# A decoder kernel's expert blocks loaded six ahead, and two GpSimd reciprocal roots moved behind the first wide product

## The chip, the cores and the metric

One Trainium2 chip, one of its cores. The metric is device time of one launch in microseconds (us). TensorE runs matmuls and transposes, VectorE and ScalarE do elementwise work and copy products out of PSUM, GpSimd does some elementwise work and issues the indirect (row by row) DMAs, SyncE (SP) issues the plain DMAs.

## What is computed

A post-norm decoder of two layers on x of 16 x 64 tokens of 128 features (1024 rows, held as 8 tiles of 128 rows). Cut to its skeleton:

```python
x = _layernorm(x + self_attention_0(x))
x = _layernorm(x + cross_attention_0(x, ctx))
x = _layernorm(x + moe(x))                 # 8 experts, the best 2 of each token
x = _layernorm(x + wide_attention(x))      # 16 heads of 64
x = _layernorm(x + cross_attention_1(x, ctx))
x = _layernorm(x + ternary_ffn(x))

def _moe_forward(x_flat):
    top_v, top_i = jax.lax.top_k(x_flat @ gate_w.T, 2)
    probs = softmax(top_v)
    for each expert e:
        hidden = silu(x_flat @ wg[e].T) * (x_flat @ wu[e].T)
        out += weight_of_e[:, None] * (hidden @ wd[e].T)
```

## The kernel before

Three parts follow each other. A first stream takes the 16 tiles of the two first attentions (`pre`), then the expert part (class `Routed`) runs, then a second stream (`post`) takes 24 tiles: 8 of the wide attention (class `Wide`), 8 of the second cross attention, 8 of the ternary feed-forward. Each engine has its own instruction queue, written out by hand; semaphores (`Mark`s) order the engines.

**The expert part.** The tokens are scattered by indirect DMA into a table in HBM, `routed_rows`, sorted by expert. 23 blocks of 128 rows are then worked off. For block j SP loads its rows into one of four buffers `XG[j % 4]` (L1458); TensorE transposes them (`block_pe`, L1472) two steps ahead of use; ScalarE copies the transpose out (L1478); GpSimd brings the expert's weights (L1488); TensorE makes the gate product (L1500, 8 instructions in the trace), the up product (L1508, 8) and, one block behind, the down product (L1531, 8); ScalarE makes the SiLU (L1516), VectorE the product of both (L1523) and the copy of the result to `YS` (L1539), and SP stores it back to `routed_rows` (L1466). At step n of its loop TensorE runs: transpose of block n+2, gate n, up n, down n-1. Some of VectorE's work on the ternary weights is put between blocks (L941 and others), after blocks 5 to 12.

SP's loop (`rows_sp`) issues four loads, then for each j: the load of block j+4, the wait for block j's copied result, the store of block j. `load(j)` waits for the transpose of block j-4, which frees the buffer.

**The gathering.** When all stores have landed, GpSimd gathers for each token tile t the two expert rows of each token (`gather`, L1662, two DMAs a tile). VectorE combines them with x and makes mean and variance (`combine`, L1670 to L1678), GpSimd makes the reciprocal root of the variance in two short instructions (`rsqrt`, L1683 and L1685), VectorE applies it (`apply`, L1690), TensorE and ScalarE turn the tile (L1698, L1703). VectorE combines and applies tiles 0 and 1 in the expert part; tiles 2 and 3, 4 and 5, 6 and 7 stand at the end of steps 1, 2 and 3 of its second stream (`post_dve`). GpSimd has all eight reciprocal roots in the expert part, ahead of its second stream.

**The second stream.** Step j of the stream holds, for the wide tiles: on TensorE the scores of tile j-2 (L835), the q and k products of tile j-1 (L808, 32 instructions in the trace), the v products of tile j-2 (L821, 16), the transposes of the probabilities P of tile j-3 (L426, 8), the product of P with V of tile j-4 (L852), then turned token tiles (L1698; tiles 4 and 5 at the end of step 3). The probabilities come about so: VectorE takes the row maximum (L400) and subtracts it (L406), ScalarE makes the exponentials (L416), VectorE sums them (L893) and takes reciprocals (L897), and GpSimd multiplies P by them (`shares_pool`, L887). This last product of tile 0 is the first wide product of P; it is GpSimd's first work in its second stream, at step 3.

Of the kernel before, what the change touches and what calls it, by code (L numbers as in the profile page):

```python
# [17 lines left out]
NT = BATCH * SEQ // P  # L18
# [14 lines left out]
BLOCKS = (2 * BATCH * SEQ + 8 * (P - 1)) // P  # L33
# [44 lines left out]
def decoder_kernel(nc, A, out):  # L78
    with ExitStack() as ctx:
# [8 lines left out]
        class Mark:  # L88
# [8 lines left out]
            def at(self, n):  # L97
                return self.sem, self.base + n

        def bc(ap, axis, n):  # L100

            shape = list(ap.shape)
            shape.insert(axis, n)
            return ap.unsqueeze(axis).to_broadcast(shape)
# [146 lines left out]
        class Transposes:  # L251
# [20 lines left out]
            def copies(self, eng, part, some=None):  # L272
                for g in some or range(len(self.groups)):
                    if g % 2 != part:
                        continue
                    _, blocks, dst = self.groups[g]
                    eng.wait_ge(self.mm, g + 1)
                    src = PS[:, self.banks[g % len(self.banks)], 0:sum(k for _, k in blocks)]
                    if part == 0:
                        eng.activation(dst, src, ACT.Copy).then_inc(self.copied[0], 1)  # L280
                    else:
                        eng.tensor_copy(dst, src).then_inc(self.copied[1], 1)
# [25 lines left out]
        class Norm:  # L308
# [18 lines left out]
            def rsqrt(self, pool, i):  # L327

                pool.wait_ge(*self.mv.at(i + 1))
                pool.tensor_scalar(ve[:, i % 2, :], mv[:, i % 2, 1:2], LN_EPS, None, ALU.add).then_inc(self.ve.sem, 1)  # L330
                pool.wait_ge(*self.ve.at(i + 1))
                pool.tensor_tensor(rstd[:, i % 2, :], ve[:, i % 2, :], half[:, :], ALU.pow).then_inc(self.rstd.sem, 1)  # L332
# [10 lines left out]
        class Stage:  # L343
# [48 lines left out]
            def rsqrt_pool(self, pool, job):  # L392
                self.norm.rsqrt(pool, job.i)
# [721 lines left out]
        def stream_of(*stages):  # L1115
            tiles = []
            for st in stages:
                for i in range(NT):
                    tiles.append(Tile(st, i, len(tiles), tiles))
            return tiles  # L1120
# [6 lines left out]
        def summed(tiles, j):  # L1127

            t, w = at(tiles, j - 5), at(tiles, j - 4)
            return w if w and w.stage.wide else t if t and not t.stage.wide else None  # L1130

        def turned(tiles, j):
            return summed(tiles, j - 1)
# [109 lines left out]
        def stream_pool(pool, tiles, extra):  # L1243
            for j in range(len(tiles) + DEPTH):
                t = at(tiles, j - 3)
                if t:
                    t.stage.shares_pool(pool, t)
                b = at(tiles, j - 1)
                if b:
                    b.stage.blocks_pool(pool, b)  # L1250
                b = at(tiles, j)
                if b:
                    b.stage.cos_pool(pool, b)
                if t:
                    t.stage.hidden_pool(pool, t)
                r = summed(tiles, j)
                if r:
                    r.stage.rsqrt_pool(pool, r)
                x = turned(tiles, j)
                if x:  # L1260
                    x.stage.bias_pool(pool, x)
                extra(pool, j)

# [3 lines left out]
        ROUTED = {0: 0, 2: 1, 4: 2, 5: 3}  # L1269


        class Routed:
# [174 lines left out]
            def rows_sp(self, sp):  # L1447

                sp.wait_ge(*self.map.at(12))
                _, at = nc.values_load_multi_w_load_instructions(  # L1450
                    bi[0:1, 1, 0:BLOCKS], engines=[mybir.EngineType.SP], min_val=0, max_val=ROWS - P,
                    skip_runtime_bounds_check_because="counts of 128 rows summed on the chip, whose largest sum ROWS holds")
                sp.wait_ge(s_sc, 16 * 2 * NT)

                def load(j):
                    if j >= 4:
                        sp.wait_ge(*self.xt_mm.at(j - 3))
                    sp.dma_start(XG[:, j % 4, :], routed[bass.ds(at[j], P), :]).then_inc(s_xg[j % 4], 16)  # L1458

                for j in range(4):  # L1460
                    load(j)
                for j in range(BLOCKS):
                    if j + 4 < BLOCKS:
                        load(j + 4)
                    sp.wait_ge(*self.ycp.at(j + 1))
                    sp.dma_start(routed[bass.ds(at[j], P), :], YS[:, j % 3, :]).then_inc(s_ys[j % 3], 16)  # L1466

# [165 lines left out]
            def pool(self, pool):  # L1633
                self.scatter(pool, len(GROUPS) - 1)
                pool.wait_ge(*self.w_cp.at(3 * EXPERTS))
                pool.wait_ge(*self.map.at(8))
                _, e = nc.values_load_multi_w_load_instructions(
                    bi[0:1, 0, 0:BLOCKS], engines=[mybir.EngineType.Pool], min_val=0, max_val=EXPERTS - 1,
                    skip_runtime_bounds_check_because="a sum of seven comparisons, each 0 or 1")
                for j in range(2, BLOCKS):  # L1640
                    self.bring_pool(pool, j, e[j])
                    if j in (6, 9, 12):
                        pool.wait_ge(s_wide, 16)
                        pool.tensor_copy(WQKV[:, j // 3 - 2, :], WRAW[:, j // 3 - 2, :]).then_inc(s_sep, 1)
                for k in range(3):
                    pool.wait_ge(s_ys[k], 16 * len(range(k, BLOCKS, 3)))
                self.gather(pool, 0)
                self.gather(pool, 1)
                self.rsqrt(pool, 0)
                self.gather(pool, 2)  # L1650
                self.rsqrt(pool, 1)
                for t in range(2, NT, 2):
                    self.gather(pool, t + 1)
                    if t + 2 < NT:
                        self.gather(pool, t + 2)
                    self.rsqrt(pool, t)
                    self.rsqrt(pool, t + 1)


            def gather(self, pool, t):  # L1660
# [49 lines left out]
        moe = Routed(a1.norm)  # L1710
# [6 lines left out]
        pre, post = stream_of(a0, a1), stream_of(wide, a2, fc)  # L1717
# [60 lines left out]
            if late and k in ROUTED:  # L1778
                moe.place(dve, ROUTED[k])

        def pre_pool(pool, j):
            k = j - DRAIN
            if k in ROUTED:
                moe.scatter(pool, ROUTED[k])

        TURNED = {(1, True): (1,), (2, True): (2, 3), (3, True): (4, 5), (4, False): (6, 7)}
# [15 lines left out]
                for t in (2 * j, 2 * j + 1):  # L1802
                    moe.apply(dve, t)

        def no_pool(pool, j):
            pass

        def load_biases(eng, b):

# [58 lines left out]
        @block.gpsimd  # L1868
        def _(pool):
            pool.memset(half[:, :], -0.5).then_inc(s_half, 1)  # L1870

            pool.memset(zero[:, :], 0.0).then_inc(s_zt, 1)
            pool.memset(VB[:, :, :, :, :, :], 0.0).then_inc(s_z, 1)
            pool.wait_ge(s_cst, 16)
            pool.wait_ge(s_z, 1)
            for b in range(2):
                for a in range(2):
                    pool.tensor_copy(VB[:, :, :, b, a, DH], bc(cst[:, C_HALF + a:C_HALF + a + 1], 1, 3).to_broadcast([P, 3, PAIRS]))\
                        .then_inc(s_z, 1)
            pool.wait_ge(s_half, 1)  # L1880
            for h in range(2):
                pool.wait_ge(s_x[h], 16)
            pool.wait_ge(s_b[0], 16 * NB)
            stream_pool(pool, pre, pre_pool)
            moe.pool(pool)
            stream_pool(pool, post, no_pool)

        @block.scalar
        def _(act):
# [51 lines left out]
```

## Time and profile before

| | us |
|---|---|
| median of 3 timed runs | 412.69 |
| lowest and highest of them | 410.81, 412.75 |
| the profiled execution's own time | 409.98 |
| span of the profile (first to last instruction) | 408.0 |
| mean granted TensorE clock | 0.946 of full |

| engine | busy us | share of the span |
|---|---|---|
| TensorE (PE) | 347.2 | 85% |
| VectorE (DVE) | 252.6 | 62% |
| GpSimd (POOL) | 186.3 | 46% |
| ScalarE (ACT) | 183.7 | 45% |

In the profile's time the expert blocks run from about 133 to 208 us, the gathering begins at 211 us, and step 3 of the second stream lies from about 240 to 258 us. A busy share is a mean over stages; the chain of waits tells which engine ended each stretch last. "Idle before" in a row is the time in which the engine stood still right before it, and the name behind the arrow is what ended that.

### The profile page before, as it was taken

To read this page: it belongs to the slowest core of one execution; us is meant where nothing else is said; L and a number is where in the kernel's file an instruction comes from. 1 tells how busy PE (TensorE), PEld (TensorE's weight loads), DVE (VectorE), ACT (ScalarE), POOL (GpSimd) and SP (SyncE) were. 2 spreads that over 40 slices of the span, in tenths; PEclk is the share of its full clock that TensorE was granted. 3 is DMA by queue.
4 is the path that set the end of the run, shared out by engine and by line. 5 is a ranking of instruction groups with operands and counts; after the bars stand their busy time and mean duration, and the time that the engine had idled before them with its cause. 6 is when DMAs were issued, how large, how long until landed. Compare 5 with 4: busy or idle time off the path is not lost.

```text
span 408.0 us, 9801 instructions
## 1 busy us (share of the span) xinstructions
PE 347.2 (85%) x3718; PEld 263.3 (65%) x3718; DVE 252.6 (62%) x592; ACT 183.7 (45%) x386; POOL 186.3 (46%) x267
## 2 busy tenths in 40 slices
PE   3889899998970899898986874899999989999892
PEld 2556666665870889898975561756667565667572
DVE  1799988896554125732353776435566567887894
ACT  2466676664672422222221251433454335667541
POOL 1767666655455245433227633102222247452673
PEclk9999999996996799999996988699999999999998
DMA  6799900000381011111111100000000000000000
GB/s 199 238 307 300 292 2 2 2 2 28 96 261 39 27 53 40 39 40 53 29 31 42 34 19 2 0 2 2 2 2 2 2 2 2 2 2 2 2 26 26
DMA packets 35938, 22.95 MB, mean 56 GB/s; under 512 B 4142, under 2 KB 33846, under 8 KB 35766
## 3 DMA queue, kind: packets, MB, share of 16 engines
q1 hardware_dynamic: 34582, 19.63, 16.7%
q0 software_dynamic: 1024, 2.10, 1.7%
q8 instruction: 30, 0.49, 0.5%
q10 hardware_dynamic: 288, 0.62, 0.5%
q14 instruction: 14, 0.11, 0.1%
HBM read 14.60 MB, written 7.73 MB: 55 GB/s over the span
## 4 chain that ended last, share of the span: by engine, by line
PE 58%; DVE 14%; issue 8%; POOL 7%; ACT 5%; DMA 5%; SPq 1%; POOLq 0%; DVEq 0%; ACTq 0%
PE banks L426 7%; PE banks L821 6%; PE banks L546 5%; PE banks L523 4%; PE banks L1500 4%; PE banks L1508 4%; PE banks L1531 4%; PE banks L808 4%; DMA XG<-routed_rows 3%; PE banks L852 3%; POOL KB L670 2%; PE banks L530 2%; DVE mx L400 2%; PE banks L495 2%; PE banks L507 2%
## 5 line engine op out<-in xcount | busy, mean ns | idle before, releaser
L330 POOL TENSOR_SCALAR ve<-mv 128x1 f32<-128x1 f32 x40 | 10.6, 265 | 93.8 <-DVE mv L325 93.8
L670 POOL TENSOR_TENSOR KB<-KT,cst 128x512 f32<-128x512 f32 x48 | 49.3, 1047 | 7.5 <-DVE KT L630 5.6
L435 ACT ACTIVATE PT<-banks 128x512 f32<-128x512 f32 x64 | 34.9, 595 | 33.3 <-PE banks L426 32.3
L1523 DVE TENSOR_TENSOR PT<-banks,PR 128x512 f32<-128x512 f32 x23 | 15.9, 691 | 46.6 <-PE banks L1508 40.0
L400 DVE TENSOR_REDUCE mx<-banks 128x16 f32<-128x1024 f32 x32 | 38.7, 1209 | 7.9 <-PE banks L530 5.6
L858 ACT ACTIVATE U<-banks 128x512 f32<-128x512 f32 x40 | 23.9, 597 | 42.5 <-PE banks L821 22.1
L426 PE MATMUL banks<-cst,PR 128*128 128x128 f32 x256 | 36.6, 289 | 6.5 <-POOL PR L887 6.5
L1488 POOL COPY U<-WALL 128x1024 f32 x21 | 21.8, 1040 | 43.8 <-PE banks L1508 42.2
L426 PEld LDWEIGHTS banks<-cst,PR 128*128 128x128 f32 x256 | 29.0, 146 | 10.2 <-POOL PR L887 7.6
L808 PE MATMUL banks<-XT,WQKV 128*128 128x128 f32 x256 | 34.9, 300 | 0.4 <-ACT XT L1703 0.4
L416 ACT ACTIVATE PR<-PR 128x1024 f32<-128x1024 f32 x32 | 33.8, 1057 | 3.1 <-DVE PR L410 2.8
L821 PE MATMUL banks<-WALL,XT 128*64 128x512 f32 x128 | 32.1, 611 | 3.3 <-DVE U L858 2.9
L808 PEld LDWEIGHTS banks<-XT,WQKV 128*128 128x128 f32 x256 | 33.1, 210 | 1.5 <-ACT XT L1703 0.7
L858 DVE COPY U<-banks 128x512 f32<-128x512 f32 x24 | 16.5, 689 | 24.7 <-PE banks L821 18.0
L523 PE MATMUL banks<-KB,QS 64*64 64x512 f32 x192 | 28.7, 651 | 2.8 <-DVE PR L410 1.5
L410 DVE TENSOR_TENSOR PR<-banks,mx 128x1024 f32<-128x1024 f32 x24 | 29.4, 1224 | 0.8
L336 DVE TENSOR_SCALAR X<-R,mv,rstd 128x128 f32<-128x128 f32 x40 | 19.2, 479 | 16.0 <-POOL rstd L332 15.9
L546 PE MATMUL banks<-VB,PT 128*64 128x18 f32 x768 | 27.0, 214 | 0.0
L546 PEld LDWEIGHTS banks<-VB,PT 128*64 128x64 f32 x768 | 24.6, 139 | 3.1 <-issue 0.6
L1500 PE MATMUL banks<-XGT,U 128*128 128x128 f32 x184 | 25.4, 283 | 0.0
L1508 PE MATMUL banks<-XGT,U 128*128 128x128 f32 x184 | 25.2, 282 | 0.0
L1531 PE MATMUL banks<-WALL,PT 128*128 x184 | 24.4, 276 | 0.6 <-DVE YS L1539 0.6
(181 smaller groups left out, 699.1 us busy)
## 6 DMA issues: line engine op xcount, KB each, us to landing
routed_rows<-zero SPq DMA_DIRECT2D x1, 4544.0 KB, 19.1
U<-in_L_ffn_wg_dram SPq DMA_DIRECT2D x8, 256.0 KB, 5.0
U<-in_L_ffn_wu_dram SPq DMA_DIRECT2D x8, 256.0 KB, 5.3
U<-in_L_ffn_wd_dram SPq DMA_DIRECT2D x8, 256.0 KB, 6.0
U<-in_L_attn_W_qkv_dram SPq DMA_DIRECT2D x1, 1536.0 KB, 22.7
XG<-routed_rows SPq DMA_DIRECT2D x23, 64.0 KB, 1.8
routed_rows<-YS SPq DMA_DIRECT2D x23, 64.0 KB, 1.6
cst<-shape_constants ACTq DMA_DIRECT2D x1, 537.0 KB, 4.6
```

The lines of the kernel that those rows point to most:

```text
L400: dve.tensor_reduce(mx[:, n % 2, :], s, AX.X, ALU.max).then_inc(self.max.sem, 1)
L426: t = pe.transpose(PS[:, B_PT + m, P * (r % 4):P * (r % 4 + 1)], PR[:, n % 2, P * r:P * (r + 1)], ident)
L435: act.activation(PT[:, n % 2, 4 * m:4 * m + 4, :].rearrange("p r q -> p (r q)"), PS[:, B_PT + m, :], ACT.Copy).then_inc(self.pt.sem, 1)
L523: pe.matmul(PS[q, B_S + g, :], QS[f, n % 3, q], KB[f, n % 2, b].rearrange("p h k -> p (h k)"), start=True, stop=False)
L546: m = pe.matmul(PS[64 * b:64 * b + 64, B_Y, w * r:w * (r + 1)], PT[:, n % 2, r, 64 * b:64 * b + 64], VB[:, n % 3, r, b].rearrange("p a e - ...
L670: pool.tensor_tensor(KB[:, n % 2, b], bc(KT[:, n % 2, b, :], 1, 8), bc(cst[:, C_HEAD:C_HEAD + 8], 2, SEQ), ALU.mult).then_inc(self.kb.sem, 1)
L808: m = pe.matmul(PS[:, bank, P * k:P * (k + 1)], WQKV[:, f // 2, P * u:P * (u + 1)], XT[:, P * i:P * (i + 1)], start=True, stop=True)
L821: m = pe.matmul(PS[64 * a:64 * a + 64, bank, :], XT[:, SEQ * (2 * i + b):SEQ * (2 * i + b + 1)], WVO[:, a, 4 * g:4 * g + 4, :].rearrange(" ...
L858: return eng.activation(o, s, ACT.Copy) if part == 0 else eng.tensor_copy(o, s)
L1500: m = pe.matmul(PS[:, j % 2, P * c:P * (c + 1)], WE[:, j % 3, 0, P * c:P * (c + 1)], XGT[:, j % 3, :], start=True, stop=True)
L1508: m = pe.matmul(PS[:, 2 + j % 2, P * c:P * (c + 1)], WE[:, j % 3, 1, P * c:P * (c + 1)], XGT[:, j % 3, :], start=True, stop=True)
L1531: m = pe.matmul(PS[:, 7, 0:P], HT[:, j % 2, c, :], WALL[:, e, 2, P * c:P * (c + 1)], start=(c == 0), stop=(c == CH - 1))
```

## The change

SP issues six loads ahead of its loop rather than four, and in the loop the load of block j+6 rather than j+4 stands in front of block j's store. The four buffers and what `load` waits for stay. GpSimd's reciprocal roots of token tiles 6 and 7 leave the expert part and stand in step 3 of the second stream, behind `shares_pool` of tile 0. For that the function that a stream calls for extra work on GpSimd is called at two places in a step, with a flag as on the other engines; what it did in the first stream stays at the late place.

```diff
@@ stream_pool
                     t.stage.shares_pool(pool, t)
+                extra(pool, j, False)
                 b = at(tiles, j - 1)
...
-                extra(pool, j)
+                extra(pool, j, True)
@@ rows_sp
-                for j in range(4):
+                for j in range(6):
                     load(j)
                 for j in range(BLOCKS):
-                    if j + 4 < BLOCKS:
-                        load(j + 4)
+                    if j + 6 < BLOCKS:
+                        load(j + 6)
                     sp.wait_ge(*self.ycp.at(j + 1))
@@ Routed.pool
                     if t + 2 < NT:
                         self.gather(pool, t + 2)
-                    self.rsqrt(pool, t)
-                    self.rsqrt(pool, t + 1)
+                        self.rsqrt(pool, t)
+                        self.rsqrt(pool, t + 1)
@@
-        def pre_pool(pool, j):
+        def pre_pool(pool, j, late):
             k = j - DRAIN
-            if k in ROUTED:
+            if late and k in ROUTED:
                 moe.scatter(pool, ROUTED[k])
@@
-        def no_pool(pool, j):
-            pass
+        def post_pool(pool, j, late):
+            if j == 3 and not late:
+                for t in (NT - 2, NT - 1):
+                    moe.rsqrt(pool, t)
```

SP's queue at the head of its block loop, before (each load is an address row and a DMA row; `block_transposed` is TensorE's transpose, `expert_output_copied` VectorE's copy of the result):

```order
L1458 DMA XG<-routed_rows 128x128
L1458 ISA [waits block_transposed]
L1458 DMA XG<-routed_rows 128x128
L1466 DMA routed_rows<-YS 128x128 [waits expert_output_copied]
L1458 ISA [waits block_transposed]
L1458 DMA XG<-routed_rows 128x128
L1466 DMA routed_rows<-YS 128x128 [waits expert_output_copied]
```

The same place after (the lines of the file are one higher):

```order
L1459 DMA XG<-routed_rows 128x128
L1459 ISA [waits block_transposed]
L1459 DMA XG<-routed_rows 128x128
L1459 ISA [waits block_transposed]
L1459 DMA XG<-routed_rows 128x128
L1459 ISA [waits block_transposed]
L1459 DMA XG<-routed_rows 128x128
L1467 DMA routed_rows<-YS 128x128 [waits expert_output_copied]
```

Ahead of the first store stand the loads of blocks 4, 5 and 6 where the load of block 4 alone stood, and from there each load is two stores earlier than it was.

GpSimd's queue from the gathers of the last token tile (tile 7) to the first wide products of P, before:

```order
L1662 DMA KB<-routed_rows,pos 128x128 x2
L1683 TENSOR_SCALAR ve8<-mv8 128x1 [waits variance_made]
L1685 TENSOR_TENSOR rstd8<-ve8,half 128x1 [waits eps_added]
L1683 TENSOR_SCALAR ve8<-mv8 128x1 [waits variance_made]
L1685 TENSOR_TENSOR rstd8<-ve8,half 128x1 [waits eps_added]
L887 TENSOR_TENSOR PR<-PR,rs 128x1024 [waits reciprocals_made] x2
```

and after:

```order
L1663 DMA KB<-routed_rows,pos 128x128 x2
L887 TENSOR_TENSOR PR<-PR,rs 128x1024 [waits reciprocals_made]
L1684 TENSOR_SCALAR ve8<-mv8 128x1 [waits variance_made]
L1686 TENSOR_TENSOR rstd8<-ve8,half 128x1 [waits eps_added]
L1684 TENSOR_SCALAR ve8<-mv8 128x1 [waits variance_made]
L1686 TENSOR_TENSOR rstd8<-ve8,half 128x1 [waits eps_added]
L887 TENSOR_TENSOR PR<-PR,rs 128x1024 [waits reciprocals_made]
```

Of the two products of P that stood behind the four short instructions, the one of tile 0 now stands ahead of them. TensorE's, VectorE's and ScalarE's queues are unchanged.

## Rows read from the trace of the kernel before

**Rows 1.** The page's chain that ended last, its shares of the span by line.

```profile
PE banks L426 7%; PE banks L821 6%; PE banks L546 5%; PE banks L523 4%; PE banks L1500 4%; PE banks L1508 4%; PE banks L1531 4%; PE banks L808 4%; DMA XG<-routed_rows 3%; PE banks L852 3%; POOL KB L670 2%; PE banks L530 2%; DVE mx L400 2%; PE banks L495 2%; PE banks L507 2%
```

**Rows 2.** Groups from 138 to 198 us: count, busy us, mean ns, idle before.

```profile
L1472 PE MATMUL banks<-cst,XG 128*128 128x128 f32 x19 | 5.8, 305 | 4.4 <-DMA XG<-routed_rows 4.4
...
L941 DVE TENSOR_SCALAR PT<-FCW,gam 128x512 f32<-128x512 f32 x2 | 3.1, 1608 | 0.0
```

**Rows 3.** Busy time by stretch: us, PE, PEld, DVE, ACT, POOL, clock, DMA share, GB/s.

```profile
138.00:198.00 60.00, 55.62 (x480) 54.01 (x480) 25.15 (x50) 16.61 (x38) 24.47 (x23) 0.99 0.15 41
```

**Rows 4.** TensorE's timeline in the blocks: start us, us, line, operation [idle before].

```profile
138.54 0.33 PE L1472 MATMUL banks<-cst,XG 128*128 128x128 f32 x1
...
141.38 0.27 PE L1472 MATMUL banks<-cst,XG 128*128 128x128 f32 x1
141.49 1.06 PE L1500 MATMUL banks<-XGT,U 128*128 128x128 f32 x8
...
143.28 1.06 PE L1531 MATMUL banks<-WALL,PT 128*128 x8
144.33 0.33 PE L1472 MATMUL banks<-cst,XG 128*128 128x128 f32 x1
...
198.29 0.33 PE L1472 MATMUL banks<-cst,XG 128*128 128x128 f32 x1
```

**Rows 5.** SP's timeline in the blocks: the load of block 5.

```profile
142.46 0.34 SPq L1458 DMA_DIRECT2D XG<-routed_rows  x1
```

**Rows 6.** The line of the block loads: from issue to landing.

```profile
DMA to landing us min/median/max: 1.7/1.8/3.4
```

**Rows 7.** Timeline of all engines around step 3 of the second stream.

```profile
237.85 0.44 PE L1698 MATMUL banks<-cst,X 128*128 128x128 f32 x1 [2.05 <-ACT XT L1703]
...
241.19 0.96 POOL L1662 DMA_INDIRECT KB<-routed_rows,pos  x1 [0.30 <-issue]
241.24 0.25 DVE L897 RECIPROCAL rs<-mx 128x16 f32<-128x16 f32 x1
...
244.44 3.87 PE L821 MATMUL banks<-WALL,XT 128*64 128x512 f32 x16
...
250.34 0.25 POOL L1683 TENSOR_SCALAR ve<-mv 128x1 f32<-128x1 f32 x1 [8.19 <-DVE mv L1678]
...
252.39 1.90 POOL L887 TENSOR_TENSOR PR<-PR,rs 128x1024 f32<-128x1024 f32 x1
252.46 1.92 DVE L1690 TENSOR_SCALAR X<-R,mv,rstd 128x128 f32<-128x128 f32 x1 [0.76 <-POOL rstd L1685]
254.35 1.97 PE L426 MATMUL banks<-cst,PR 128*128 128x128 f32 x8 [6.03 <-POOL PR L887]
...
258.58 1.99 PE L835 MATMUL banks<-U 64*64 64x64 f32 x64
...
264.86 3.87 PE L821 MATMUL banks<-WALL,XT 128*64 128x512 f32 x16
```

**Rows 8.** The line of `apply`: duration ns min/median/max.

```profile
L1690 DVE TENSOR_SCALAR X<-R,mv,rstd x8: 345/371/1915, 217.3 to 252.5; 128x128 f32<-128x128 f32 x8
```

**Rows 9.** Timeline of all engines two steps on, at steps 4 and 5.

```profile
272.02 1.09 PE L426 MATMUL banks<-cst,PR 128*128 128x128 f32 x8
...
273.05 1.16 PE L835 MATMUL banks<-U 64*64 64x64 f32 x64
...
276.44 1.90 POOL L887 TENSOR_TENSOR PR<-PR,rs 128x1024 f32<-128x1024 f32 x1 [2.50 <-DVE rs L897]
...
277.47 1.23 DVE L406 TENSOR_TENSOR PR<-banks,mx 128x1024 f32<-128x1024 f32 x1
278.02 1.08 PE L821 MATMUL banks<-WALL,XT 128*64 128x512 f32 x4
```

**Rows 10.** Busy time by stretch, columns as in rows 3: PE and its clock.

```profile
238.00:239.00 1.00, 1.00 (x29) 0.78 (x32) 0.85 (x4) 0.28 (x1) 0.79 (x2) 0.50 0.00 0
...
249.00:250.00 1.00, 0.00 (x0) 0.00 (x0) 0.93 (x4) 0.00 (x0) 0.00 (x0) 1.00 0.00 0
...
276.00:288.00 12.00, 11.76 (x154) 8.28 (x153) 6.79 (x12) 5.06 (x9) 2.69 (x3) 1.00 0.01 3
```

More of the change, by code:

```diff
@@ L1885, in _ @@
             moe.pool(pool)
-            stream_pool(pool, post, no_pool)
+            stream_pool(pool, post, post_pool)
         @block.scalar
```

## The prediction

> **What bounds the kernel now.** I read the chain that ended last first: TensorE's lines lead it, but one DMA has 3% of the span, some 12 us, the loads of the expert blocks [rows 1]. So the blocks come next, from 138 to 198 us. TensorE is busy 55.62 of 60.00 us there at full clock (0.99), VectorE 25.15, ScalarE 16.61, GpSimd 24.47 [rows 3]; no engine but TensorE is near its limit, and what holds TensorE up is named in its group of transposes: 4.4 us idle until a load had landed [rows 2]. The second place is step 3 of the second stream. TensorE's v products end at 244.44 + 3.87 = 248.31, and its next work, the transposes of P of wide tile 0, starts at 254.35 after 6.03 us of idleness that GpSimd's product of P ended [rows 7]. That product started at 252.39. Its own input, the reciprocals on VectorE, was ready at 241.24 + 0.25 = 241.49 [rows 7]. What held GpSimd was the instruction ahead in its queue: the reciprocal root of token tile 6 waited 8.19 us for the variance, made by VectorE only at 250.3, since VectorE combines tiles 6 and 7 at the end of step 3 [rows 7]. TensorE thus waited for a small piece of work that neither it nor the product needs.
>
> **Part 1, the loads.** Removed: nothing. Moved: each load, past two stores on SP's queue. Without a wait TensorE needs per block 0.11 us for the transpose (141.38 to 141.49) and 0.895 us for each of three products (141.49 to 143.28 holds two), 2.79 us together [rows 4]. The down product that starts at 143.28 is over by 144.17, yet the next transpose starts at 144.33: its load was issued at 142.46, 1.87 us earlier, and a load lands after 1.8 us in the median [rows 4 to 6]. So even the loads that seem to be on time are late by 0.1 to 0.2 us, and one that takes 3.4 us costs the whole excess [rows 6]. From the transpose of block 3 at 138.54 to that of block 22 at 198.29 are 19 blocks in 59.75 us; 19 x 2.79 = 53.0, so 6.7 us are lost [rows 4]. I take off 0.4 us, an estimate for the small ternary product that stands in there once and for transposes that start a little slower: **6.3 us** come back. The bounds are 4.4 us (the idle time that the group names) and 6.7 us.
>
> Does the new place give enough lead? Load j+6 is issued where load j+4 was, and is needed two blocks later: 1.87 + 2 x 2.79 = 7.45 us of lead, against 3.4 us for the slowest landing seen [rows 4 to 6]. Its wait, the transpose of block j+2, is passed by then: TensorE makes it at step j, and SP gets to this load only behind the store of block j-1, whose down product is also step j's last. So the added wait holds no store back, and the stores queued behind it keep their time. What is late next? VectorE has the ternary weights between blocks, two instructions of 3.1 us together [rows 2], longer than one block. Its mean without these two is (25.15 - 3.1) / 20, 1.1 us a block [rows 2, 3], so two blocks need 3.1 + 2.2 = 5.3 us of 5.58: it fits, barely, and may cost some tenths; the lower bound of 4.4 us covers that. The last stores, the gathers and all that follows hang on the last down product and move up with it.
>
> **Part 2, the reciprocal roots.** The four short instructions stay, 0.25 us and the like each; they go behind the product of P, and that takes 1.90 us [rows 7]. GpSimd is free of its last gather at 241.19 + 0.96 = 242.15, has the reciprocals since 241.49, and ends the product near 244.1. TensorE comes to the transposes of P at 248.31, 4 us later, so GpSimd is out of the way. What is late next is then the chain inside step 3: transposes of P, two copies on ScalarE, the exponentials of tile 1, the turned token tiles 4 and 5 (TensorE waits for ScalarE's copy of the one before it can make the other, as one step earlier, 2.05 us idle [rows 7]), and the scores of tile 2. In the trace this takes 258.58 - 254.35 = 4.23 us [rows 7]; the transposes ran at half clock there, 1.97 us against 1.09 at full clock [rows 9], so I put 4.23 - 0.88 = 3.35 us. The clock was still full (1.00) at 249 to 250 [rows 10]. The scores of tile 2 then start at 248.31 + 3.35 = 251.7 rather than 258.58: **6.9 us** come back. The bounds: 6.0 us (should the chain take its 4.23) and 7.3 us.
>
> Does VectorE follow? It is done with combining both tiles and applying tile 6 by 252.46 - 0.76 = 251.70 and applies tile 7 from 252.46, as before [rows 7]. In the trace that took 1.92 us beside GpSimd's product, against a median of 0.37 [rows 7, 8]. After the change no product runs there and it is over at 252.85. Then tile 1's sum and reciprocals and tile 2's maximum and subtraction (L893, L897, L400, L406; 0.25 and 1.23 us by [rows 7, 9], the sum and the maximum taken as long as the subtraction, an estimate) end near 256.8. The second v product of tile 2 needs VectorE's copy behind these, by about 251.7 + 4.97 + 1.08 = 257.8 (score start to first v product and its length, [rows 9]); the copy fits with little to spare. If VectorE's 1.92 us stayed, TensorE would lose about 1 us. From there each stage runs at TensorE's pace, 11.76 us busy of 12.00 [rows 10], and the gain has nothing to vanish into.
>
> The Trainium skill (SBUF — State Buffer, section Who interferes with whom) has it that VectorE and GpSimd share one port pair, and that whoever holds it blocks the other for its whole instruction, if the VectorE instruction has two SBUF inputs or runs in a two-port mode. By that page the moved product sets `apply` free and holds up none of its new neighbours, as the subtraction reads PSUM. The trace agrees: the subtraction took 1.23 us fully beside a product of 1.90 us, and the product kept its length [rows 9]. Were every VectorE instruction blocked, the product of tile 0 would delay VectorE by under 2 us at 242 us, where ScalarE needs the result only some 6 us later, and that of tile 1 would cost TensorE some 1.5 us.
>
> **The clock.** Scores to first v product of tile 2 took 264.86 - 258.58 = 6.28 us after the long idleness, at half clock in part, against 278.02 - 273.05 = 4.97 at full clock [rows 7, 9]: 1.3 us to win if the clock stays up. The idleness left in step 3 is some 1.7 us. The nearest row is that of one step earlier: 2.05 us idle, then clock 0.50 [rows 7, 10]. It is a little longer, so I take half, **0.6 us**, bounds 0 and 1.3. Moving the idle stretches may also lengthen or shorten the other half-clock stretches, an estimate of 1.5 us either way.
>
> **The sum.** 6.3 + 6.9 + 0.6 = 13.8 us. Against the profiled execution's own 409.98 (span 408.0 and 1.98 around it) that gives 396.2 us. The timed runs' median, 412.69, lies 2.7 us above that execution, and all three are above it; carried over, the time is **398.9 us**.
>
> **Rivals.**
> 1. A new wait takes a part of the gain: VectorE, packed in step 3 and between the blocks, becomes the one that is waited for. For it: the margins above are of 0.3 to 1 us, and VectorE is busy 0.93 us of the one from 249 to 250 [rows 10]. Against it: it is under half busy in the blocks [rows 3]. Price: part 1 at 4.4, part 2 down to 4, no clock gain, sum 8.4: 404.3 us.
> 2. The loads go on holding TensorE, because their landing time is no constant but grows with the loads and stores that are in flight together. Then part 2 alone pays: 412.69 - 7.5 = 405.2 us. Against it: the lead grows fourfold.
> 3. The change doesn't do what it says, or both waits hide others of equal length (TensorE's wait for the product of P might hide a second one, for ScalarE): within 2 us of 412.7. Against it: the reciprocals were 10.9 us old when the product of P began, and nothing else in TensorE's queue changes place.
> 4. Slower: the stores. A load now lies between stores whose landing frees the three `YS` buffers and at the end releases the gathers. Were loads and stores together to land in over 7.45 us, TensorE would wait again at each block, for the excess. To eat the 7.5 us of part 2 over 17 blocks it takes 0.44 us each, a landing of 7.9 us, and for 2.5 us more than before 8.0 us, over four times the median [rows 6]: 415 us.
>
> **How the numbers follow.** The forecast has 0.74 (395 to 402), rival 1 0.12, rival 2 0.07, rival 3 0.04, rival 4 0.03. The low end is the sum's upper bounds, 6.7 + 7.3 + 1.3 = 15.3, and 0.5 to 1.5 us of clock elsewhere, set against a value between 409.98 and 412.69: 394.5 us. The high end takes in rival 1: 404.5 us. A measurement of this kernel tells a change of over 0.5%, 2.1 us, from none. Faster by more than that: 0.93; within 0.5%: 0.04; slower by more: 0.03.
>
> **What the changed profile would show.** Part 1: the block transposes have no idle time before them that ends with a load, apart from the first; each block takes 2.8 us; loads are issued some 7 us before their transpose. Part 2: the product of P of tile 0 starts some 10 us before the combining of tile 6 ends; the transposes of P follow the v products without a gap; `apply` of tile 7 takes 0.4 us; the clock at half rate appears, if at all, only behind the turned tiles. I am wrong if TensorE's idle time in step 3 reappears under VectorE's or ScalarE's name, or if the blocks stay at 2.9 us and more with another releaser.

## The result

| | before | changed |
|---|---|---|
| timed runs, median (lowest to highest), us | 411.75 (408.19 to 412.75) | 394.88 (394.38 to 395.17) |
| profiled execution's own time, us | 409.98 | 394.38 |
| span of the profile, us | 408.0 | 392.4 |
| mean granted TensorE clock | 0.946 | 0.960 |

The ratio is 0.960, with a 95% interval of 0.954 to 0.967: 4.0% less. 398.9 us was forecast, 3.3% less, with a range from 394.5 to 404.5. In three later comparisons, where the kernel before takes 415.5 to 418.0 us, the same pair gave 0.966, 0.967 and 0.965 (below). So 3.4% is what the change gives as a rule, which is about the 13.8 us that were forecast; the first comparison had some 2 us more, and the ledger below shows from where.

The page's chain by line, for [rows 1] (from the expert part on, lines of the changed file are one higher), no longer has the block loads:

```profile
PE banks L426 7%; PE banks L821 6%; PE banks L546 6%; PE banks L1501 5%; PE banks L1509 5%; PE banks L1532 5%; PE banks L523 5%; PE banks L852 3%; DVE mx L400 3%; PE banks L808 3%; PE banks L495 2%; PE banks L530 2%; PE banks L507 2%; DVE mx L893 2%; PE banks L1308 2%
```

The blocks first. The group of VectorE's two ternary instructions from 138 to 192 us (columns as in [rows 2]):

```profile
L941 DVE TENSOR_SCALAR PT<-FCW,gam 128x512 f32<-128x512 f32 x2 | 3.1, 1608 | 0.0
```

They are as long as before. The view of the tile `XG` shows the block transposes of the whole kernel (duration ns min/median/max, first and last start us; then idle time by releaser, with its count):

```profile
L1473 PE MATMUL banks<-cst,XG x23: 272/273/476, 131.2 to 189.6; 128*128 128x128 f32 x23
its engine sat idle before it (us, times) until:
  DMA XG<-routed_rows: 17.6, 4
  ACT XGT L1479: 0.9, 2
...
DMA to landing us min/median/max: 1.7/1.8/3.1
```

The median transpose takes 273 ns where rows of 0.33 us stood between those of 0.27 [rows 4], and landing has the median that it had [rows 6]. The 17.6 us (counted on the weight side and on the matmul side) lie ahead of the first three blocks, when the scatter has just ended. TensorE's timeline shows the pace (start us, us, line, operation):

```profile
136.38 0.27 PE L1473 MATMUL banks<-cst,XG 128*128 128x128 f32 x1
...
139.17 0.27 PE L1473 MATMUL banks<-cst,XG 128*128 128x128 f32 x1
...
189.62 0.27 PE L1473 MATMUL banks<-cst,XG 128*128 128x128 f32 x1
```

From block 3 to block 22 it is 189.62 - 136.38 = 53.24 us, against 59.75 [rows 4]; one block takes 2.79 us. SP issues a load long ahead:

```profile
140.25 0.34 SPq L1459 DMA_DIRECT2D XG<-routed_rows  x1
```

That is the load of block 7. Block 7 is transposed four blocks after the one at 136.38, at 147.54: 7.3 us of lead where there were 1.87 us [rows 5]. The wait that this load adds holds no store back, as the rows of the second store show:

```profile
142.16 0.29 DVE L1540 COPY YS<-banks 128x128 f32<-128x128 f32 x1
...
142.48 0.36 SPq L1467 DMA_DIRECT2D routed_rows<-YS  x1
```

VectorE's copy of the result ends at 142.45, and the store leaves 0.03 us later.

Step 3 of the second stream in the changed kernel, all engines:

```profile
232.06 0.96 POOL L1663 DMA_INDIRECT KB<-routed_rows,pos  x1 [0.30 <-issue]
232.10 0.25 DVE L897 RECIPROCAL rs<-mx 128x16 f32<-128x16 f32 x1
...
233.04 1.91 POOL L887 TENSOR_TENSOR PR<-PR,rs 128x1024 f32<-128x1024 f32 x1
...
233.47 1.23 DVE L406 TENSOR_TENSOR PR<-banks,mx 128x1024 f32<-128x1024 f32 x1
...
235.34 2.95 PE L821 MATMUL banks<-WALL,XT 128*64 128x512 f32 x12 [0.34 <-DVE U L858]
...
238.22 1.09 PE L426 MATMUL banks<-cst,PR 128*128 128x128 f32 x8
...
240.31 0.25 POOL L1684 TENSOR_SCALAR ve<-mv 128x1 f32<-128x1 f32 x1 [5.36 <-DVE mv L1679]
...
241.25 0.30 PE L1699 MATMUL banks<-cst,X 128*128 128x128 f32 x1 [1.83 <-ACT XT L1704]
...
241.53 1.82 PE L835 MATMUL banks<-U 64*64 64x64 f32 x64
...
242.44 0.34 DVE L1691 TENSOR_SCALAR X<-R,mv,rstd 128x128 f32<-128x128 f32 x1 [0.77 <-POOL rstd L1686]
243.29 4.86 PE L808 MATMUL banks<-XT,WQKV 128*128 128x128 f32 x32
...
248.07 3.87 PE L821 MATMUL banks<-WALL,XT 128*64 128x512 f32 x16
```

GpSimd makes its product right behind the last gather, from 233.04 to 234.95, and 3.3 us later TensorE transposes P straight behind its v products, with no idle time where 6.03 us stood [rows 7]. The reciprocal root of tile 6 still waits for VectorE (5.36 us), but now nobody waits for it. `apply` of tile 7 takes 0.34 us where it took 1.92. What is late next is in the rows too: TensorE waits 1.83 us for ScalarE's copy of a turned tile.

**The ledger.** Start times of the same instruction in both profiles, and how far the changed kernel is ahead there:

| place | before | changed | ahead by | won or lost since the row above |
|---|---|---|---|---|
| transpose of block 0 | 133.03 | 131.23 | 1.80 | 1.80, ahead of the blocks |
| transpose of block 3 | 138.54 | 136.38 | 2.16 | 0.36, half clock over sooner |
| transpose of block 22 | 198.29 | 189.62 | 8.67 | **6.51, the blocks** |
| scores of wide tile 0 | 225.89 | 216.75 | 9.14 | 0.47, mostly half clock over sooner |
| end of step 3's v products | 248.31 | 238.29 | 10.02 | 0.88, mostly no half clock in steps 2 and 3 |
| scores of wide tile 2 | 258.58 | 241.53 | 17.05 | **7.03, step 3** |
| v products of wide tile 2 | 264.86 | 248.07 | 16.79 | -0.26, half clock in both |
| last product of P with V | 341.30 | 324.50 | 16.80 | 0.01 |
| first ternary transposes | 383.13 | 367.19 | 15.94 | -0.86, half clock in the changed one |
| last ternary product | 401.52 | 385.91 | 15.61 | -0.33, mostly the rest of it |

The two bold rows make 13.5 us of the 15.6; the others are the start and the clock.

### The profile page after: what moved, and what is told of

It is laid out like the page before. It is cut to its first block, busy times and chain, and to the rows that moved or that the text cites. A ratio compares the mean times of both kernels' runs of the same rounds, so it can differ in the third digit from the quotient of the medians.

```text
span 392.4 us, 9801 instructions
## 1 busy us (share of the span) xinstructions
PE 341.5 (87%) x3718; PEld 260.5 (66%) x3718; DVE 250.7 (64%) x592; ACT 183.8 (47%) x386; POOL 186.8 (48%) x267
## 4 chain that ended last, share of the span: by engine, by line
PE 63%; DVE 18%; issue 6%; ACT 5%; POOL 3%; DMA 2%; SPq 1%; POOLq 0%; DVEq 0%; ACTq 0%
PE banks L426 7%; PE banks L821 6%; PE banks L546 6%; PE banks L1501 5%; PE banks L1509 5%; PE banks L1532 5%; PE banks L523 5%; PE banks L852 3%; DVE mx L400 3%; PE banks L808 3%; PE banks L495 2%; PE banks L530 2%; PE banks L507 2%; DVE mx L893 2%; PE banks L1308 2%
## 5 line engine op out<-in xcount | busy, mean ns | idle before, releaser
L426 PE MATMUL banks<-cst,PR 128*128 128x128 f32 x256 | 35.7, 284 | 0.5 <-POOL PR L887 0.5
L336 DVE TENSOR_SCALAR X<-R,mv,rstd 128x128 f32<-128x128 f32 x40 | 19.6, 490 | 17.3 <-POOL rstd L332 17.3
L523 PE MATMUL banks<-KB,QS 64*64 64x512 f32 x192 | 27.4, 614 | 3.1 <-issue 1.5
L1501 PE MATMUL banks<-XGT,U 128*128 128x128 f32 x184 | 25.3, 282 | 0.0
L332 POOL TENSOR_TENSOR rstd<-ve,half 128x1 f32<-128x1 f32 x40 | 23.3, 583 | 3.3
```

The lines of the kernel that those rows point to most:

```text
L426: t = pe.transpose(PS[:, B_PT + m, P * (r % 4):P * (r % 4 + 1)], PR[:, n % 2, P * r:P * (r + 1)], ident)
L523: pe.matmul(PS[q, B_S + g, :], QS[f, n % 3, q], KB[f, n % 2, b].rearrange("p h k -> p (h k)"), start=True, stop=False)
L1501: m = pe.matmul(PS[:, j % 2, P * c:P * (c + 1)], WE[:, j % 3, 0, P * c:P * (c + 1)], XGT[:, j % 3, :], start=True, stop=True)
```

## The experiments

Each was profiled once and timed beside the kernel before on its own chip. "Blocks" is the time from the transpose of block 3 to that of block 22; "idle" is TensorE's idle time ahead of the transposes of P of tile 0.

| kernel | median us | the kernel before, median us | ratio (95%) | blocks | idle |
|---|---|---|---|---|---|
| before, first profile | 411.75 | | | 59.75 | 6.03 |
| before, second profile | 419.57 (one run) | 416.87 | | 59.84 | 6.03 |
| changed | 394.88 | 411.75 | 0.960 (0.954 to 0.967) | 53.24 | none |
| changed, 2nd | 403.34 | 418.0 | 0.966 (0.960 to 0.972) | 54.23 | none |
| changed, 3rd | 403.35 | 416.87 | 0.967 (0.960 to 0.974) | 54.26 | none |
| changed, 4th | 401.39 | 415.5 | 0.965 (0.960 to 0.970) | 53.23 | none |
| loads only | 410.81 | 418.0 | 0.988 (0.980 to 0.996) | 53.23 | 6.03 |
| roots only | 407.62 | 418.0 | 0.978 (0.972 to 0.985) | 59.18 | none |
| loads five ahead | 403.72 | 418.0 | 0.969 (0.962 to 0.975) | 54.26 | none |
| loads eight ahead | 403.45 | 416.87 | 0.970 (0.962 to 0.978) | 53.23 | none |
| turned tiles split | 399.96 | 416.87 | 0.959 (0.952 to 0.966) | 53.92 | none |
| split, again | 399.89 | 415.5 | 0.960 (0.954 to 0.966) | 53.27 | none |
| split, copies on ScalarE | 394.07 | 415.5 | 0.949 (0.943 to 0.955) | 53.24 | none |

The theory (A): two separate waits, each an order in a queue, were taken away, and their gains add. The rivals are named in the expectations.

### Loads only, roots only

```diff
-                for j in range(4):
+                for j in range(6):
                     load(j)
                 for j in range(BLOCKS):
-                    if j + 4 < BLOCKS:
-                        load(j + 4)
+                    if j + 6 < BLOCKS:
+                        load(j + 6)
```

> The kernel before with the loads six ahead and nothing else. Theory A (the two waits are separate and add): the blocks lose all idle time, from the transpose of block 3 to that of block 22 it takes 53.2 us instead of 59.75, and TensorE keeps its 6 us of idleness in step 3 under the name of GpSimd's product of P; 6.5 us less than the kernel before, ratio 0.984. Rival B (the parts pay only together, since what follows absorbs an earlier start): the blocks shrink all the same, but less than 4 us arrive at the end, ratio above 0.990.

And the changed kernel with four loads ahead as before, so that only the reciprocal roots are moved:

```diff
-                for j in range(6):
+                for j in range(4):
                     load(j)
                 for j in range(BLOCKS):
-                    if j + 6 < BLOCKS:
-                        load(j + 6)
+                    if j + 4 < BLOCKS:
+                        load(j + 4)
```

> The kernel before with only the two reciprocal roots moved behind the first wide product of P. Theory A: the block loads keep their 4 to 5 us of named idleness, the 6 us in step 3 go, and the scores of tile 2 follow the v products of tile 1 by some 3.3 us; 7 to 9 us less, by how the clock falls, ratio 0.978 to 0.983. Rival B: below 4 us, above 0.990. The rival that the port, not the queue, stretched the application of tile 7: it would stay at 1.92 us; by theory A it takes under 0.45 us, since no product of GpSimd runs beside it.

Groups over the whole of the kernel with the loads alone:

```profile
L426 PE MATMUL banks<-cst,PR 128*128 128x128 f32 x256 | 36.2, 286 | 6.5 <-POOL PR L887 6.5
...
L1472 PE MATMUL banks<-cst,XG 128*128 128x128 f32 x23 | 6.8, 297 | 8.9 <-DMA XG<-routed_rows 8.0 <-ACT XGT L1478 0.9
```

and of the kernel with the roots alone:

```profile
L426 PE MATMUL banks<-cst,PR 128*128 128x128 f32 x256 | 35.7, 284 | 0.5 <-POOL PR L887 0.5
...
L1473 PE MATMUL banks<-cst,XG 128*128 128x128 f32 x23 | 7.6, 332 | 11.7 <-DMA XG<-routed_rows 10.8 <-ACT XGT L1479 0.9
...
L1691 DVE TENSOR_SCALAR X<-R,mv,rstd 128x128 f32<-128x128 f32 x8 | 2.9, 366 | 5.2 <-POOL rstd L1686 5.2
```

Each part takes away its own wait and leaves the other's: the wait for GpSimd's product (6.5 against 0.5 us; 0.5 us of it belongs to a later tile) and the wait for loads (10.8 us with the first block's, 8.0 us without the rest). The times agree with a sum: 1.2% and 2.2% less, together 3.4% (good to about 1 point), and both parts together gave 3.4% on the same chip. The loads alone gave 5 us by the ratio and 7 by the medians where 6.5 were expected, with an interval from 1.7 to 8.4 us. So by the times rival B, under 4 us for each, is out for the roots but not for the loads.

The traces settle the rest. From the transpose of block 22 to the end of the span it takes 202.8 us with the roots alone, and 202.4 to 202.8 us in the six profiles that also have five, six or eight loads ahead: what the blocks win arrives at the end whole. With the roots where they were it is 209.7 and 212.3 us in the two profiles of the kernel before and 210.1 us with the loads alone. Rival B is out for the loads too. What the blocks win is not a fixed number, though: with the roots alone they took 59.18 us, 0.9 of it from half clock between blocks 3 and 4, so the late loads cost 5.0 us there and 6.5 in the first profile. With the roots alone `apply` takes 366 ns in the mean of eight and none over 0.41 us; with the loads alone its longest is 1.91 us again. So it was the product of GpSimd beside it that stretched it; GpSimd's queue order only put the two side by side.

### The changed kernel again

> The changed kernel once more, to see which parts of the 15.6 us of span repeat. Theory A: the blocks' 53.2 us and the missing idle time in step 3 repeat to a few hundredths; the stretches at half clock (wide q and k products, steps 2 and 3, the first ternary tiles) and the start ahead of the blocks differ by up to 2 us. If the 1.8 us won ahead of the blocks repeat, they belong to the change and I have missed a cause. Ratio 0.955 to 0.970.

> The changed kernel beside the next ones on the same chip. Expected by theory A: ratio 0.955 to 0.970, block transposes 2.79 us apart, no idle time ahead of the transposes of P of tile 0.

> The changed kernel as the measure for the next two on the same chip: ratio 0.955 to 0.970.

The ratio was 0.966, 0.967 and 0.965. The missing idle time repeats. In the second and third the blocks took 1.0 us more than 53.23, all of it in the one interval from block 3 to block 4 (3.78 and 3.81 us in place of 2.79), which ran at half clock; in the kernel with the roots alone that interval was 3.70. The 1.8 us ahead of the blocks do not repeat: the first transpose came at 131.2 us in the first profile of the changed kernel and at 139.7, 139.3 and 137.8 in the others, where the kernel before had it at 133.0 and 139.9. That is a scatter larger than 1.8 us in both kernels, so nothing gives them to the change. Scores to first v product of tile 2 took 6.54, 4.98, 6.50 and 6.54 us: at half clock in part in three of four.

### How far ahead must a load be?

```diff
-                for j in range(6):
+                for j in range(5):
...
-                    if j + 6 < BLOCKS:
-                        load(j + 6)
+                    if j + 5 < BLOCKS:
+                        load(j + 5)
```

> The changed kernel with the loads five ahead instead of six. Lead by the trace: 1.87 + 2.79 = 4.66 us, against a slowest landing of 3.4 us. Theory A (any lead above the slowest landing hides it): no transpose waits for a load and the time is that of the changed kernel, within 1.5 us. Rival C (the landing time grows with what is in flight and the sixth is needed): some idle time with the loads' name comes back, 1 to 4 us, and with it the time.

The same with eight in place of five:

> The changed kernel with the loads eight ahead. The wait of load j+8 is for the transpose of block j+4, which TensorE makes at step j+2, so that it is not yet passed when SP comes to it, and block j's store stands behind it for about one more block. Theory A: the loads are early enough anyway, the stores have three buffers of slack, and the last eight blocks have no load ahead of their stores; so the time is that of the changed kernel, within 1 us. Rival D (a wait in front of the store is what limits how far ahead one may load): VectorE's copy into the three result buffers waits for stores, TensorE's down products with it, 0.5 us and more a block, 8 us and more in all.

Five ahead: 403.72 us, beside 403.34 for six on the same chip, with the interval from block to block 2.79 us as with six, and the slowest landing again 3.4 us. Rival C is out; one block more of lead than before would have done. Eight ahead: 403.45 us beside 403.35. SP's timeline of that kernel shows the wait in front of the stores that was to be tested (start us, us):

```profile
148.66 0.38 SPq L1467 DMA_DIRECT2D routed_rows<-YS  x1
151.01 0.34 SPq L1459 DMA_DIRECT2D XG<-routed_rows  x1
151.44 0.38 SPq L1467 DMA_DIRECT2D routed_rows<-YS  x1
```

and VectorE's and TensorE's the work that the second store and the load before it wait for:

```profile
150.57 0.27 PE L1473 MATMUL banks<-cst,XG 128*128 128x128 f32 x1
150.78 0.29 DVE L1540 COPY YS<-banks 128x128 f32<-128x128 f32 x1
```

The load waits for the transpose, which ends at 150.84, and leaves at 151.01; the store stands behind it and leaves at 151.44. But VectorE's copy of its result was done only at 151.07, so the wait holds the store back by 0.37 us, where a store of the changed kernel leaves 0.03 us after its copy, and not by about one block as the expectation has it. TensorE does not feel these 0.3 us: blocks 53.23 us. A delay of a whole block, which is what rival D is about, was not tried, and the rival stays open for it.

### What is late next, first try

TensorE's idle time left in steps 2 and 3 comes from the order around the turned token tiles.

```diff
-        TURNED = {(1, True): (1,), (2, True): (2, 3), (3, True): (4, 5), (4, False): (6, 7)}
+        TURNED = {(1, True): (1,), (2, False): (2,), (2, True): (3,), (3, False): (4,), (3, True): (5,), (4, False): (6, 7)}
```

> The changed kernel with one of the two turned token tiles of steps 2 and 3 (tiles 2 and 4) made at the early place of the step, ahead of the copies of P and the exponentials on ScalarE. In the changed kernel TensorE is idle 2.05 us in step 2 and 1.83 us in step 3, since its second turned tile waits for ScalarE's copy of the first, which stands behind the exponentials. Theory A (that queue order is what is late next, now that GpSimd is out of the way): both idle times shrink to under 0.5 us, the half-clock stretch behind step 3 goes too, 3 to 4.5 us less than the changed kernel, ratio to the kernel before 0.945 to 0.962. Rival E (VectorE's subtraction and copies are just as late): under 1.5 us, and VectorE's name ahead of TensorE's idle time.

> The kernel with tiles 2 and 4 turned at the early place once more, since its first profile fell on the longest of its runs: TensorE waited 1.94 us for VectorE's copy of the last q and k product in step 3 and then ran at half clock. If that wait is of the program it is there again (1.9 to 2.0 us), half clock behind it or not; if it was chance it is under 0.8 us. Time 3 to 4.5 us less than the changed kernel.

3.4 us less than the changed kernel beside it on one chip (403.35 us) and 1.5 us less on the other (401.39 us). TensorE's timeline in the second profile:

```profile
236.91 0.30 PE L1699 MATMUL banks<-cst,X 128*128 128x128 f32 x1 [0.46 <-ACT XT L1704]
...
245.13 2.95 PE L821 MATMUL banks<-WALL,XT 128*64 128x512 f32 x12 [1.93 <-DVE U L858]
...
248.18 1.04 PE L426 MATMUL banks<-cst,PR 128*128 128x128 f32 x8
249.05 0.27 PE L1699 MATMUL banks<-cst,X 128*128 128x128 f32 x1
249.25 1.16 PE L835 MATMUL banks<-U 64*64 64x64 f32 x64
...
256.97 2.95 PE L821 MATMUL banks<-WALL,XT 128*64 128x512 f32 x12 [1.66 <-DVE U L858]
```

2.05 us became 0.46, 1.83 us became nothing, and the scores follow the transposes of P by 1.07 us rather than 3.3. But 1.9 us come back under VectorE's name: TensorE now waits for its copy of the fourth q and k product of tile 2. The first profile had 1.94 us at the same place, and TensorE at half clock behind it (12 instructions 4.49 us, not 2.95). So the wait is of the program and the half clock is not. One step later stands a second one, 1.66 us at 256.97 (1.67 in the first profile), where the changed kernel has no wait. Together they eat what was won in steps 3 and 4: from the scores of tile 1 to those of tile 3 it takes 27.1 us (237.14 to 264.23), against 27.3 in the changed kernel beside it. What is left is step 2, 2.05 - 0.46 = 1.6 us, about the 1.5 us of that chip; the other 1.9 us of the 3.4 no trace here divides. Both theories were right in part: the idle time for ScalarE went, and VectorE was nearly as late.

### What is late next, second try

```diff
-        DVE_FILLS = [0, 0, 0, 1, 0, 1, 0, 1]
+        DVE_FILLS = [0, 0, 0, 0, 0, 1, 0, 1]
```

ScalarE copies the fourth q and k product of every wide tile; the rest is the split kernel.

> The split kernel in which ScalarE rather than VectorE copies the fourth q and k product of each wide tile. Theory E (in step 3 VectorE's queue, combining two tiles and then sum, maximum and subtraction, is what is late next): the 1.94 us go, and the 0.2 to 0.7 us of TensorE's idle time with VectorE's copy as releaser in each of the other steps as well, 2 to 4.5 us less than the split kernel. Rival F (the copy only was the messenger; ScalarE's own queue, exponentials and four copies, is then as late): under 1 us, with ScalarE's name ahead of the idle time.

394.07 us, 5.8 us less than the split kernel and 7.3 us less than the changed kernel beside it: more than expected. TensorE's timeline:

```profile
238.87 2.86 PE L821 MATMUL banks<-WALL,XT 128*64 128x512 f32 x12
241.89 1.08 PE L821 MATMUL banks<-WALL,XT 128*64 128x512 f32 x4 [0.17 <-DVE U L858]
242.90 0.33 PE L1699 MATMUL banks<-cst,X 128*128 128x128 f32 x1
243.07 1.04 PE L426 MATMUL banks<-cst,PR 128*128 128x128 f32 x8
...
249.12 3.88 PE L821 MATMUL banks<-WALL,XT 128*64 128x512 f32 x16
```

and a whole wide step of this kernel, busy time by stretch, columns as in [rows 3]:

```profile
256.00:268.00 12.00, 12.00 (x161) 8.54 (x157) 6.28 (x11) 5.62 (x9) 2.69 (x3) 1.00 0.01 1
```

The 1.93 us are down to 0.17, the 1.66 us of step 4 are gone (249.12, 16 instructions without a wait), and TensorE is busy 12.00 of 12.00 us where it was 11.76 before [rows 10]. A wide step takes 11.70 us rather than 12.07 (from one product of P with V to the next). The start times of the split kernel and of this one, both from the same chip, divide the gain behind the blocks: 0.6 us up to the scores of tile 1, 1.85 from there to the scores of tile 2 (12.11 against 10.26 us), 1.8 to those of tile 3 (14.98 against 13.16), 1.6 from there to the end; 5.8 us in all, as the times have it. The expectation fell short because it had the wait of step 3 alone and not the one of step 4. Rival F is out: TensorE waits for ScalarE no longer than in the split kernel (from 224 to 340 us 1.7 us in both). This version beats both kernels.

## Why the prediction was right

**What bounds it.** Right at both places: each wait, taken away alone, is gone from the trace, and the time follows.

**Part 1.** 6.3 us forecast, 6.51 measured in the first pair. The late loads cost somewhat less in two other profiles, 6.2 us in the second one of the kernel before and 5.0 us in the one with the roots alone (59.84 and 59.18 us, less the 0.4 and 0.9 us that half clock adds between blocks 3 and 4); all are inside the bounds of 4.4 and 6.7 us. The period of 2.79 us worked out from single rows is the measured one. I took 0.4 us off for slower transposes and the small ternary product; the trace has only the second, as one interval of 3.01 us: 0.2 us. The slower transposes were themselves late loads. The lead of 7.45 us was 7.3. VectorE between the blocks cost nothing: behind its two long instructions the intervals are 2.79, 2.79 and 2.81 us. The wait that the load adds held no store back (0.03 us from copy to store), and one that holds each store back by 0.37 us (eight ahead) costs nothing either.

**Part 2.** 6.9 us forecast, 7.03 measured. The chain inside step 3 was put at 3.35 us and took 241.53 - 238.22 = 3.31. GpSimd's product ended 3.3 us before TensorE asked for it, not 4. VectorE did follow. Whether it would have with `apply` still at 1.92 us was not tried, so that the end of the stretching was needed is an argument. That the margins there were thin was right as well: take the next idle time away and VectorE's copy is what ends TensorE's wait. One reading was wrong: in [rows 9] the subtraction does not lie fully beside GpSimd's product, since it runs from 277.47 to 278.70 and the product ends at 278.34. The changed kernel has such a pair, the subtraction from 233.47 to 234.70 within the product from 233.04 to 234.95, and there it takes 1.23 us as well; the conclusion holds.

**The clock.** This term was mis-sized. I put 0.6 us for a clock that might stay up behind step 3; it was -0.26. In seven profiles that have the roots moved and the turned tiles where they were, scores to first v product of tile 2 took 6.50 to 6.54 us six times and 4.98 once. The row one step earlier was thus the better guide than the middle that I took: the lower bound, 0, was the value to forecast.

**The sum.** 13.8 us were forecast. The terms that repeat make 13.5, and three more comparisons gave 3.4%, 13.5 to 14.7 us of 415 to 418. The 15.6 us of the first pair of profiles hold 2.1 us more, from the start ahead of the blocks (1.8), and from half-clock stretches that fell shorter in three places and longer in two. I had put the stretches at 1.5 us either way and had no term for the start.

The time itself came out 4.0 us below 398.9 and only 0.4 us inside the range. Of the 4.0 us, 1.8 are the profiles' (15.6 against 13.8). The other 2.2 come from the step from profile to median: I carried over that the timed runs of the kernel before lay 2.7 us above its profiled execution, and in the changed kernel they lie 0.5 us above (394.88 against 394.38). Three runs were too few for that term, for a fourth of the kernel before took 408.19 us, 1.8 us below the profiled one. The mechanism and both large terms were right; that the first time fell inside the range, with these two pulling the same way, owes something to luck.

## What to carry to other kernels

Where an engine's idle time names a releaser, look at what stood ahead of the releasing instruction in its own queue, and whether its inputs had long been there: here they were 10.9 us old, and moving four short instructions behind one gave 7 us. For a transfer compare its lead with the slowest landing and not with the median: loads that seemed just in time cost 0.1 to 0.2 us each and a slow one its whole excess, and one block more of lead ended both. After each such move read who is late next; TensorE's idle time in step 3 went from GpSimd's name to ScalarE's and then to VectorE's, and each step was worth its own experiment. And when an experiment is to make something late, read from the rows how late it became: the loads eight ahead were meant to hold a store back by a block and did so by 0.37 us.

## What the runs showed of the hardware

- VectorE's `apply` of tile 7, a `tensor_scalar` with SBUF in and out, started 0.07 us after a GpSimd product over 128x1024 from SBUF and took 1.92, 1.91 and 1.91 us in the three profiles with that order (twice the kernel before, once the loads alone); each time it ended 0.08 or 0.09 us after the product. Every other `apply`, in all thirteen profiles, took 0.34 to 0.41 us. GpSimd's product kept its 1.90 us. VectorE's subtraction out of PSUM, fully within such a product, kept its 1.23 us. How long the instruction is stretched follows the product: another `tensor_scalar` of the same shape (L336, 0.36 us in the median) started 0.07 us after a GpSimd product of 1.04 us over 128x512 and took 1.05 us, so that it too ended 0.08 us after the product (kernel before):

```profile
339.59 1.04 POOL L670 TENSOR_TENSOR KB<-KT,cst 128x512 f32<-128x512 f32 x1
339.66 1.05 DVE L336 TENSOR_SCALAR X<-R,mv,rstd 128x128 f32<-128x128 f32 x1 [1.56 <-POOL rstd L332]
```

- After 2.05 us of TensorE idleness in step 2 the clock was at half rate in the kernel before (1.2 of 2.4 GHz, 0.50 in [rows 10]) and stayed full in the first profile of the changed one. That is no difference of the kernels: in the second profile of the changed kernel, behind the same 2.05 us, the scores took 1.99 us, the length at half clock, and not 1.16. A profile of one execution doesn't tell what such a stretch costs. Here is the changed kernel in its first profile right after the same idleness, still at full clock, and then behind the 1.83 us of step 3 at half:

```profile
228.00:229.00 1.00, 0.29 (x5) 0.20 (x7) 0.90 (x4) 0.56 (x2) 0.50 (x2) 1.00 0.00 0
...
242.00:243.00 1.00, 1.00 (x48) 1.00 (x44) 0.56 (x2) 0.00 (x0) 0.40 (x1) 0.50 0.07 16
```

- The kernel before took 411.75 us in the first comparison and 415.5 to 418.0 us in the later ones (two chips; whether one of them is that of the first comparison is not on record). The profiles have most of the difference ahead of the expert blocks, where the change touches nothing: the first block transpose comes 6.9 us later in the second profile of the kernel before, and 6.5 to 8.4 us later in those of the changed kernel. So only ratios against runs made beside each other can be compared.
